# LoRA-style adapters in a 128-sequence residual layer: A and B of all eight adapters turned, split and stored once instead of once per adapter

## The reference, cut to what matters

```python
# x: (128, 64, 512) f32; w: (8, 64, 64); W: (512, 512); A: (8, 16, 512); Bm: (8, 512, 16)
w = L0_cond_weights[itok_B_0_7]; b = fside_8xS_0[itok_B_0_7]
x = x + einsum('bct,bcd->bdt', x, w) + b[:, :, None]                # layer 0: a weight per sequence
H = einsum('btd,od->bto', x, W)                                     # layer 1: one W for all
xa = einsum('btd,brd->btr', x, A[itok_B_0_6])                       # ... and an adapter per sequence
delta = einsum('btr,bor->bto', xa, Bm[itok_B_0_6]) * scalings[itok_B_0_6]
x = x + H + delta
```

## Time and profile before

| | us |
|---|---|
| median of 3 runs | 246.33 (245.89 to 246.4) |
| the profiled execution | 246.09 |
| its span, first to last instruction | 244.4 |
| TensorE busy | 231.5 |
| VectorE busy | 149.0 |
| ScalarE busy | 109.8 |
| GpSimd busy | 72.1 |

### The profile page before, as it was taken

The page is one execution under the profiler, slowest core; times in us unless marked ns, Lnnn a source line. Parts: engine busy times, 40 slices in busy tenths (PEclk is TensorE's granted clock), DMA queues, the critical chain, the costliest instruction groups (busy, mean ns, idle before and its releaser), DMA issues.

```text
span 244.4 us, 9841 instructions
## 1 busy us (share of the span) xinstructions
PE 231.5 (95%) x2916; PEld 189.2 (77%) x2917; DVE 149.0 (61%) x258; ACT 109.8 (45%) x191; POOL 72.1 (30%) x280
## 2 busy tenths in 40 slices
PE   1989999999999999999999999999999999999792
PEld 1777888888887888888888888888788888888561
DVE  6778856774457736675357836675467844344662
ACT  3265462552535353562526353463526443425451
POOL 3456602560046301560046300655134231000000
PEclk9999999999999999999999999999999999999999
DMA  6846664745465563745455563646545473642133
GB/s 145 265 130 149 176 178 127 216 115 169 132 182 139 157 188 109 212 113 186 131 151 159 144 206 103 202 118 185 151 132 168 132 208 98 195 123 71 46 86 89
DMA packets 23621, 36.56 MB, mean 150 GB/s; under 512 B 6066, under 2 KB 6066, under 8 KB 23602
## 3 DMA queue, kind: packets, MB, share of 16 engines
q1 hardware_dynamic: 16544, 26.36, 39.0%
q10 hardware_dynamic: 7058, 9.97, 13.7%
HBM read 19.53 MB, written 16.78 MB: 149 GB/s over the span
## 4 chain that ended last, share of the span: by engine, by line
PE 83%; DVE 7%; ACTq 2%; ACT 2%; issue 2%; DMA 2%; POOL 0%; SPq 0%; DVEq 0%; POOLq 0%
PE ps L860 65%; PE ps L829 13%; PE ps L805 3%; DMA x_ring<-in_x_dram 2%; DVE x_lo L527 1%; ACTq L680 1%; PE ps L764 1%; ACTq L237 1%; DVE o_ring L547 1%; ACT x_hi L645 1%; DVE o_ring L542 1%; DVE m_lo L510 1%; DVE x L519 1%; DVE last_parts L532 1%; ACT m_f L667 0%
## 5 line engine op out<-in xcount | busy, mean ns | idle before, releaser
L860 PE MATMUL ps<-m_hi,x_hi 128*128 x248 | 99.1, 400 | 0.0
L860 PE MATMUL ps<-m_hi,x_lo 128*128 x248 | 96.8, 390 | 0.0
L860 PE MATMUL ps<-m_lo,x_hi 128*128 x248 | 96.7, 390 | 0.0
L527 DVE TENSOR_TENSOR x_lo<-x,x_hi 128x512 fp32r<-128x512 f32 x64 | 44.4, 694 | 65.1 <-ACT x_hi L645 65.0
L368 POOL COPY p_pair<-p_all 64x64 f32 x128 | 41.3, 323 | 125.8 <-DVE x L519 93.3
L645 ACT ACTIVATE x_hi<-x 128x512 fp32r<-128x512 f32 x64 | 40.4, 631 | 56.7 <-ACT o_ring L658 26.8
L658 ACT ACTIVATE o_ring<-ps 128x512 f32<-128x512 f32 x60 | 35.8, 596 | 54.9 <-PE ps L860 54.7
L860 PEld LDWEIGHTS ps<-m_hi,x_hi 128*128 128x128 f32 x248 | 46.5, 188 | 10.6 <-issue 0.3
L860 PEld LDWEIGHTS ps<-m_hi,x_lo 128*128 128x128 f32 x248 | 46.5, 188 | 10.0
L860 PEld LDWEIGHTS ps<-m_lo,x_hi 128*128 128x128 f32 x248 | 46.6, 188 | 9.0
L519 DVE TENSOR_TENSOR x<-ps,bias_pair 128x512 f32<-128x512 f32 x64 | 43.8, 686 | 7.7 <-PE ps L829 6.3
(11 more groups left out here) (99 smaller groups left out, 83.8 us busy)
## 6 DMA issues: line engine op xcount, KB each, us to landing
x_ring<-in_x_dram SPq DMA_DIRECT2D x124, 128.0 KB, 2.7
out_dram<-o_ring ACTq DMA_DIRECT2D x64, 128.0 KB, 2.6
out_dram<-o_ring SPq DMA_DIRECT2D x64, 128.0 KB, 2.3
a_f<-in_L_cond_A_dram SPq DMA_DIRECT2D x8, 128.0 KB
o_ring<-in_L_cond_W_dram SPq DMA_DIRECT2D x2, 256.0 KB, 4.2
o_ring<-in_L_cond_W_dram ACTq DMA_DIRECT2D x2, 256.0 KB, 5.2
x_ring<-in_x_dram ACTq DMA_DIRECT2D x4, 128.0 KB, 3.2
b_nat<-in_L_cond_Bm_dram ACTq DMA_DIRECT2D x1, 256.0 KB, 3.7
```

The source lines that it names most:

```text
L527: nc.vector.tensor_tensor(x1_lo[:, u % HELD], x1[:, u % 2], x1_hi[:, u % HELD], ALU.subtract).then_inc(x1_lo_ready, 1)
L860: mm = nc.tensor.matmul(ps[:, 2 + u % 2, :], part, m_tile(m, k, c), start=(c == 0 and part is hi and m is m_hi), stop=(c == TC - 1 and par ...
```

## The change

The adapters of places 0 and 1 are built as before, with their rows in another order (row r of an adapter, then its four copies by turns, instead of copy by copy). For places 2 to 7:

- SP loads A of all eight adapters as one block of 128 rows (256 KB), at its step 0. GpSimd scales all of B at once at its step 7. TensorE turns it (`turn_all`, four transposes) at pair 4. ScalarE rounds and VectorE splits both, at pair 4, into `a_all` and `b_all`.
- SP writes the parts to memory at its step 5 (`store_parts`), each row twice: four DMAs of 512 KB, 2.10 MB in all, ahead of pair 5's store and of the next `load_quad`.
- SP fetches the finished `a_parts` and `b_parts` of a place as one block each, 2 x 128 KB (`load_parts`), at step 7 for place 2 (this waits until all four stores have landed) and at u = 4 of each loop body for places 3 to 7. The products of place 2 stand after layer 1 of pairs 9 and 10, two at a time; those of places 3 to 7 stand where they were, at u = 6, 7, 0, 1.
- In the loop `dup_b`, `turn_b`, `a_round`, `b_round`, `a_split` and `b_split` are gone. Twelve pairs are written out ahead of a loop of five bodies.
- The factors `neg` are made by four small VectorE instructions behind the zeroing of `b_dup`; before, GpSimd made them with five of its own.

```diff
-    HEAD = 4
+    HEAD = 12
     BODY = 8
-    BODIES = 6
+    BODIES = 5
...
         def tiles_of(j, u, n):
...
             if n is not None:
-                return {6: [(n + 2, 0)], 7: [(n + 2, 1)], 0: [(n + 2, 2)], 1: [(n + 2, 3)]}.get(u, [])
-            return {1: [(1, 0), (1, 1)], 2: [(1, 2), (1, 3)]}.get(j, [])
+                return {6: [(n + 3, 0)], 7: [(n + 3, 1)], 0: [(n + 3, 2)], 1: [(n + 3, 3)]}.get(u, [])
+            return {1: [(1, 0), (1, 1)], 2: [(1, 2), (1, 3)],
+                    9: [(2, 0), (2, 1)], 10: [(2, 2), (2, 3)]}.get(j, [])
...
+            def store_parts():
+
+                sp.wait_ge(all_split, 2)
+                for part in range(2):
+                    sp.dma_start(a_dram.rearrange("k r g t -> (k r) g t")[:, 2 * part:2 * part + 2],
+                                 a_all[:, part].bitcast(F32).unsqueeze(1).to_broadcast([P, 2, T])).then_inc(parts_out, 16)
+                for part in range(2):
+                    sp.dma_start(b_dram.rearrange("k r (d q) t -> q (k r) d t", q=2)[part],
+                                 b_all[:, part].bitcast(F32).unsqueeze(1).to_broadcast([P, 2, T])).then_inc(parts_out, 16)
+
+            def load_parts(i):
+
+                k, = words(sp, regs[:1], order[0:1, ds(i, 1)], K - 1)
+                sp.wait_ge(parts_out, 64)
+                sp.wait_ge(m_summed, i * TC)
+                sp.dma_start(a_parts[0:GR, :].bitcast(F32), a_dram[ds(k, 1)]
+                             .rearrange("k r g t -> (k r g) t")).then_inc(parts_in, 16)
+                sp.dma_start(b_parts[0:GR, :].bitcast(F32), b_dram[ds(k, 1)]
+                             .rearrange("k r g t -> (k r g) t")).then_inc(parts_in, 16)
...
             def step(j, u, n):
-                if n is not None and u == 0:
-
-                    load_a(n + 2)
+                if n is None and j == 0:
+                    sp.wait_ge(a_ready, 2)
+                    sp.dma_start(a_f[:], A.rearrange("k r t -> (k r) t")).then_inc(a_in, 16)
+                if n is None and j == 5:
+                    store_parts()
+                if n is None and j == 7:
+                    load_parts(2)
+                if n is not None and u == 4:
+                    load_parts(n + 3)
                 if u % L0_QUAD == 2 and (not isinstance(j, int) or j + XR + 2 < PAIRS):
                     load_quad(j + XR + 2)
...
             nc.vector.memset(b_dup[:], 0.0).then_inc(zeroed, 1)
 
+            bits = [did(nc.vector.tensor_scalar(bits_i[:, part:part + 1], pid_i[:], 2 - part, None, ALU.bitwise_and))
+                    for part in range(2)]
+            need(bits[1])
+            for part in range(2):
+                nc.vector.tensor_scalar(neg[:, part:part + 1], bits_i[:, part:part + 1], -0.5 - 0.5 * part, None,
+                                        ALU.mult).then_inc(zeroed, 1)
...
-                if n is not None and u == HEAD + 1:
-                    a_split(n + 2)
-                    b_split(n + 2)
+                if n is None and j == 4:
+                    dve.wait_ge(all_rounded, 1)
+                    nc.vector.tensor_tensor(a_all[:, 1], a_f[:], a_all[:, 0], ALU.subtract).then_inc(all_split, 1)
+                    dve.wait_ge(all_rounded, 2)
+                    nc.vector.tensor_tensor(b_all[:, 1], b_turned_at(2), b_all[:, 0], ALU.subtract).then_inc(all_split, 1)
...
-                if n is not None and u == HEAD:
-                    a_round(n + 2)
-                    b_round(n + 2)
+                if n is None and j == 4:
+                    act.wait_ge(a_in, 48)
+                    nc.scalar.activation(a_all[:, 0], a_f[:], ACT.Copy).then_inc(all_rounded, 1)
+                    act.wait_ge(b_all_turned, 1)
+                    nc.scalar.activation(b_all[:, 0], b_turned_at(2), ACT.Copy).then_inc(all_rounded, 1)
...
-                if n is not None and u == HEAD:
-                    turn_b(n + 2)
-                if n is not None and u == HEAD + 2:
-
-                    pe.wait_ge(m_ready, n * TC + 2 * TC)
+                if n is None and j == 4:
+                    turn_all()
+                if n is not None and u == 6:
+
+                    pe.wait_ge(m_ready, n * TC + 3 * TC)
...
                 for place_at, chunk in tiles_of(j, u, n):
 
-                    pe.wait_ge(a_ready, place_at + 1)
-                    pe.wait_ge(b_ready, place_at + 1)
+                    if isinstance(place_at, int) and place_at == 1:
+                        pe.wait_ge(a_ready, 2)
+                        pe.wait_ge(b_ready, 2)
+                    else:
+                        pe.wait_ge(parts_in, place_at * 32 - 32)
                     m_product(place_at * TC + chunk, chunk)
```

More of the change, by code:

```diff
@@ L211, in pairs @@
             for j in range(head):
-                step(j, j, None)
+                step(j, j % BODY, None)
             with eng.Fori(0, BODIES) as n:
@@ L301, in step @@
                              o_ring[0:C, u % OR, :]).then_inc(even_out[u % OR], 16)
-            pairs(sp, step, 0)
+            pairs(sp, step)
             for slot in range(OR):
@@ L380, in step @@
                                           .rearrange("p s d -> p (s d)")).then_inc(pair_ready, 1)
-                if n is None and j == HEAD - 1:
+                if n is None and j == 3:
                     dup_b(1)
                     pool.wait_ge(b_dupped, 2)
-                if n is not None and u == 7:
-                    dup_b(n + 2)
-                    pool.wait_ge(b_dupped, n + 3)
+                if n is None and j == 7:
+                    pool.wait_ge(b_turned, 2)
+                    nc.gpsimd.tensor_tensor(b_dup[:].rearrange("p c r g -> p c (r g)").rearrange("p c (k r) -> p c k r", k=K), b_nat[:].rearrange("p k (c r) -> p c k r", c=TC),
+                                            scal_all[:].unsqueeze(1).unsqueeze(3).to_broadcast([P, TC, K, R]),
+                                            ALU.mult).then_inc(b_all_scaled, 1)
+                    pool.wait_ge(b_all_scaled, 1)
             pairs(pool, step)
@@ L484, in a_split @@
                 dve.wait_ge(a_rounded, i + 1)
-                nc.vector.scalar_tensor_tensor(out=a_parts[0:GR, :], in0=a_parts[0:GR, :], scalar=neg[0:GR, 0:1], in1=a_f[:],
+                nc.vector.scalar_tensor_tensor(out=a_parts[0:GR, :], in0=a_parts[0:GR, :], scalar=neg[0:GR, 0:1], in1=a_f[0:GR, :],
                                                op0=ALU.mult, op1=ALU.add).then_inc(a_ready, 1)
@@ L764, in turn_b, with turn_all @@
                     mm = nc.tensor.transpose(ps[:, b_bank(i), c * P:c * P + P],
-                                             b_dup[:, c].rearrange("p g r -> p (g r)"), ident[:])
+                                             b_dup[:, c].rearrange("p r g -> p (r g)"), ident[:])
                 mm.then_inc(b_turned, 1)
+            def turn_all():
+                pe.wait_ge(b_all_scaled, 1)
+                pe.wait_ge(m_added, TC - 1)
+                for c in range(TC):
+                    mm = nc.tensor.transpose(ps[:, b_bank(2), c * P:c * P + P],
+                                             b_dup[:, c].rearrange("p r g -> p (r g)"), ident[:])
+                mm.then_inc(b_all_turned, 1)
             pe.wait_ge(firsts_ready, 1)
```

56 lines of the change are left out of this document (28 added, 28 removed).

## The result

The changed kernel takes 250.19 us, the median of four runs (248.92 to 251.24); the kernel before took 246.11 on the same chip. The ratio is 1.015, with a 95% interval of 1.0127 to 1.0173: slower, by 4.1 us, where 1.3 us faster was forecast (245.0 against 246.33). The profiled execution is the fastest of the four, with 248.92 us and a span of 247.2. It is 2.8 us longer than the profiled one of before, so what its trace shows covers about two thirds of the difference of the medians; a second profile, further down, is 4.1 us longer and shows where the rest lies.

A forecast was written before the change was run, and what follows sets the result against it. TensorE was taken to bound the kernel: -2.2 us for five sets of transposes, +0.4 for the beginning, +0.5 for the parts' wait, -1.3 in sum, giving a median of 245.0 us. The 8-in-10 range was 244.0 to 247.0.

The forecast's parts named there:

- the landing of place 2's parts: Ahead of place 2's first product, after layer 1 of pair 9: TensorE waits 0.5 us, bounds 0 and 2.9.
- the order in a ring: SP's queue: descriptors consumed in order, so stores delay whatever SP issues behind them; spoke against the change, no separate size.
- rival "slower": Pairs 9 and 10: stores ahead of x and parts in SP's queue hold TensorE over 2.3 us; 247.4 us, chance 0.13.
- The loop: Places 3 to 7: TensorE's transposes of B leave its chain, saving 0.44 us each; five sets give 2.2 us.
- The beginning: Before the sorting: four small VectorE instructions delay the x load behind it, costing 0.4 us, bounds 0 and 0.45.
- the beginning costs nothing: Rival at the first x load: x waits on memory and the parts are in time; -2.2, 244.1 us, chance 0.08.

The follow-up runs named there:

- the filler: The change plus 14 idle TensorE products ahead of place 2's first product, inside its wait; 248.76 us, ratio 1.0039 to the kernel before.
- each row once: The change with every row of the parts stored once, two stores of 512 KB in place of four; 247.75 us, ratio 0.9992 to the kernel before.
- the last kernel: The change with GpSimd issuing part stores (rows not doubled) and fetches, and A split and stored one pair earlier; 244.35 us, ratio 0.9911 to the kernel before.

## Why the prediction was wrong, point by point

- **The step that failed** is the landing of place 2's parts. The prediction let SP issue its four stores "from 36.4" and had the eight loads of x follow "no later" than before, because "four issues at near 0.65 us each" would fit in. Then it took the landing from bytes and a rate, 37.7 + 4.19 MB / rate + 1.0, and a wait of 0.5 us (0 to 2.9). Measured: a wait of 3.25 and, in a second profile, 4.05 us. The issues of L293 took 1.18 each, the register loads behind them up to 1.60, the next store's issue 1.00, and the first x was 3.5 us late. From then on the DMA engines weren't full, so no rate set the landing: the parts took the usual 2.75 us from an issue that came late. The small stores (bytes away, instructions kept) and the stores on GpSimd (instructions away from SP, bytes kept) divide the 3.54 us: 1.9 to 2.1 are the bytes in flight, which slow SP's own work, and 1.5 to 1.7 are the four issues, which the prediction had fit in at no cost.
- **The Trainium skill** ("DMA: Bandwidth & Descriptors", Queues, rings and completion order) was weighed for the order in a ring. When the parts were fetched, nothing of the stores was left ahead of them: they took 2.75 us from their issue, against 2.9 in the median. With the stores on GpSimd, SP had none of them ahead of it and TensorE waited all the same. So the ring's order isn't what cost most. The same page (Latency and other measured facts) gives a register load a floor of about 0.6 us; here the short ones take 0.28 in the stretches with room and 2.03 with the engines full, so the traces don't bear out the floor.
- **The rival "slower"** had the right place and sign, at a chance of 0.13, but rested on the rate as well, and had 247.4. No sum had the clock in it: a wait of that length also costs what comes behind it. 1.7 us here by the chain, 1.1 to 2.0 by the filler's run. The idle time of the bound engine was priced at its length, and that was too little.
- **The loop.** 0.44 a body was forecast, 0.36 measured, and the layer 1 of four pairs without a piece between (11.16) is what the prediction said. The mechanism was right, 5 x 0.44 = 2.2 became about 1.9. The parts of places 3 to 7 never made anything wait.
- **The beginning** was to cost 0.4. `ones_b` starts at 2.46 and not 2.64 (2.20 before). Layer 0 of pair 0 started at 11.29, 1.24 earlier than before and not 0.4 later, for two reasons that were not in the sum: its x had landed less than 3 us after the issue, where the kernel before waited for it until 12.48 (3.99 us), and the transposes of W ahead of it took 341 ns in the mean and not 421. The rival "the beginning costs nothing" had named the first of them. Most of this was lost again in the 0.89 us at 22.32. With rows and factors alone the time is that of before, so the term is 0, the low end of its bounds.
- **Writing out twelve pairs** was priced at nothing. It may cost 0.6 us. The gap at 22.32 us ("issue") isn't that cost: it stands in several of the variants and in the best one (0.94), but also where nothing is written out (0.63, with rows and factors alone), and it is absent from two variants that are (the filler, each row once). Layer 0 of pairs 4 to 7 starts between 23.2 and 24.1 in all of them, whether the products ahead end at 22.3 or at 23.5, so it waits for something else. What that is wasn't tried.

What stays open: why layer 1 of pair 9 ends 0.82 us later in one profile of the change than in the other, the cost of the written-out body, and what layer 0 of pairs 4 to 7 waits for.

## What to carry to other kernels

A transfer that is off the critical path isn't free. Its issues take time in the list of the engine that issues loads, and while it fills the DMA engines that engine's register loads are slow, whichever queue the bytes are in. Find a stretch where the DMA share is low and send it there, in pieces, from an engine that nobody waits for; then look at when the next load of the busy queue is *issued*, before working out any rate. And price a wait of TensorE, where it bounds the kernel, at more than its length: behind those of 2.35 to 4.05 us here the clock fell too.

## What the runs showed of the hardware

- SP's register loads took 0.28 us in the median in every trace. Behind the stores, with a DMA share near or above 1, one took 1.60, 1.86 or 2.03; the longest in the kernel before was 1.01 and in the last kernel 0.55. Its issues of 128 KB took 0.47 in the median. One of 1.78 stood in the full stretch, but single long ones stand elsewhere too (1.34 in the kernel before, at a share of 0.31, and 1.84 in the last kernel, at 0.73), so full engines aren't their only cause.
- TensorE's waits of 2.35, 2.78, 3.25 and 4.05 us were followed by a granted clock of 0.50, the 1.2 GHz level, for some 3 us (four profiles); after waits of 0.83 and 1.74 it stayed at 1.00. The Trainium skill ("TensorE: Matmul & The Clock Gate", Part 1: The HAM clock gate) says that the array runs at 1.2 GHz when it was idle; these rows agree.
- Products whose `x_hi` and `x_lo` tiles lie 32 bytes off a multiple of 64 take 404 and 396 ns instead of 400 and 390: 4 us of this kernel, from one unused tile of 8 bytes. The products read `m_hi` and `m_lo` too, but these lie ahead of the tile and did not move. Which of the moved tiles does it wasn't separated.
- The transposes of W at the beginning have two durations, with the granted clock at 1.00 in both traces: in the group of before 421 ns in the mean, in that of the change 341, because in the latter they got short part of the way. What switches them isn't known.

```profile
L751 PE MATMUL ps<-ident,o_ring 128*128 128x128 f32 x16 | 3.9, 421 | 0.0
```

```profile
L790 PE MATMUL ps<-ident,o_ring 128*128 128x128 f32 x16 | 2.9, 341 | 0.0
```
